# Products that keep TensorE streaming, 64-column relative scores, row norms on ScalarE and a q/k/v scratch with its channels outermost

## What is computed

```
x = x + window_attention(layernorm(x))     # windows of 14x14, 12 heads of 16, relative scores of rows and columns
t = t + experts(layernorm(t))              # softmax router, 2 of 8 experts, 192 -> 768 -> 192, exact gelu
x = x + dilated_attention(layernorm(x))    # 3x3 neighbours at dilations 1, 2 and 3, 4 groups, heads of 16
t = t + experts(layernorm(t))

# in the window attention, with q reshaped to (windows*heads, 14, 14, 16):
rel_h = einsum('bhwc,hkc->bhwk', q, Rh)    # Rh[h, k] depends on the row h inside its window
rel_w = einsum('bhwc,wkc->bhwk', q, Rw)
attn  = softmax(q @ k.T * scale + rel_h[..., None] + rel_w[..., None, :])
```

## Time and profile before

| | us |
|---|---|
| median of 3 runs (927.88 to 931.53) | 928.06 |
| the profiled execution | 926.22 |
| its span, first to last instruction | 924.4 |
| TensorE busy | 761.4 (82%) |
| VectorE, GpSimd, ScalarE busy | 427.2, 367.6, 297.6 |
| mean granted clock | 0.876 |

### The profile page before, as it was taken

The page is one execution under the profiler, slowest core; times in us unless marked ns, Lnnn a source line. Parts: engine busy times, 40 slices in busy tenths (PEclk is TensorE's granted clock), DMA queues, the critical chain, the costliest instruction groups (busy, mean ns, idle before and its releaser), DMA issues.

```text
span 924.4 us, 19239 instructions
## 1 busy us (share of the span) xinstructions
PE 761.4 (82%) x6098; PEld 668.5 (72%) x6099; DVE 427.2 (46%) x1007; ACT 297.6 (32%) x830; POOL 367.6 (40%) x795
## 2 busy tenths in 40 slices
PE   2999999999891999999981648997682799999990
PEld 1787888888680899999971427883672699999990
DVE  7105545557628333333326305998247433333324
ACT  3222545445523333333331330011210233333330
POOL 5753353330211566666640040000040566676640
PEclk9665899999975899999995778999755899999996
DMA  7382565564581111111103159400861111111115
GB/s 215 104 227 71 127 143 125 141 150 88 173 309 62 45 45 50 44 48 50 50 23 137 30 141 275 68 23 23 301 261 64 40 53 47 47 50 49 46 30 204
DMA packets 63186, 96.51 MB, mean 104 GB/s; under 512 B 28551, under 2 KB 46684, under 8 KB 63136
## 3 DMA queue, kind: packets, MB, share of 16 engines
q1 hardware_dynamic: 42208, 59.60, 22.7%
q0 software_dynamic: 20928, 36.25, 13.1%
HBM read 65.51 MB, written 31.52 MB: 105 GB/s over the span
## 4 chain that ended last, share of the span: by engine, by line
PE 64%; DVE 16%; DMA 6%; issue 5%; POOL 4%; ACT 2%; SPq 1%; DVEq 0%; POOLq 0%
PE ps L1367 14%; PE ps L1375 10%; PE ps L1379 6%; PE ps L735 5%; DMA qkvd<-arena 3%; PE ps L717 3%; PE ps L761 3%; DVE x_sb L1316 2%; PE ps L374 2%; PE ps L745 2%; PE ps L1358 2%; PE ps L1764 2%; PE ps L1746 2%; PE ps L781 2%; DVE arena L1660 2%
## 5 line engine op out<-in xcount | busy, mean ns | idle before, releaser
L1409 ACT ACTIVATE arena<-ps,b1s 128x128 f32<-128x128 f32 x468 | 129.5, 376 | 256.9 <-PE ps L1379 254.1
L1367 PE MATMUL ps<-arena 128*128 x936 | 165.4, 327 | 1.5 <-DVE rt L1281 1.5
L1367 PEld LDWEIGHTS ps<-arena 128*128 128x128 f32 x936 | 150.3, 190 | 2.4 <-issue 2.1
L1375 PE MATMUL ps<-xnT 128*128 128x128 f32 x936 | 120.1, 279 | 3.5 <-DVE xnT L1274 3.5
L1375 PEld LDWEIGHTS ps<-xnT 128*128 128x128 f32 x936 | 116.8, 195 | 4.8 <-DVE xnT L1274 4.8
L270 POOL TENSOR_TENSOR rstd<-veps,cst 128x8 f32<-128x8 f32 (+2 forms) x6 | 10.0, 1659 | 205.0 <-DVE veps L264 205.0
L597 DVE TENSOR_REDUCE rt<-ps 98x2 f32<-98x392 f32 x96 | 52.8, 561 | 78.8 <-PE ps L761 78.8
L1423 POOL TENSOR_TENSOR credit<-credit 1x1 f32<-1x1 f32 x306 | 58.1, 190 | 78.0 <-DVE rt L1281 33.4
L1431 POOL DMA_INDIRECT xnT<-xnd,gcur x78 | 79.1, 1014 | 16.3 <-issue 14.9
L1379 PE MATMUL ps<-xnT,rt 64*128 64x128 f32 x936 | 73.7, 290 | 0.0
L983 ACT ACTIVATE arena<-ps 98x392 f32<-98x392 f32 x96 | 46.9, 499 | 78.4 <-PE ps L781 77.7
(11 more groups left out here) (199 smaller groups left out, 1249.8 us busy)
## 6 DMA issues: line engine op xcount, KB each, us to landing
arena<-in_w SPq DMA_DIRECT2D x16, 576.0 KB, 8.6
arena<-in_w1a SPq DMA_DIRECT2D x16, 384.0 KB, 6.3
arena<-yd SPq DMA_DIRECT2D x8, 768.0 KB, 6.8
kk<-kd SPq DMA_DIRECT2D x48, 96.0 KB
qq<-qd SPq DMA_DIRECT2D x16, 264.0 KB
qd<-arena POOLq DMA_DIRECT2D x16, 224.0 KB, 5.3
qq<-qd SPq DMA_DIRECT2D x16, 192.0 KB
arena<-in_w1b SPq DMA_DIRECT2D x16, 192.0 KB, 6.9
```

Source lines behind the costliest of these rows:

```text
L1367: last = mm(ps[:, DOWN, 0:C], hidT[r][:, f, :], w2s[:, e, f, :], start=f == 0, stop=f == FT - 1)
L1375: mm(hidden(r, f), wcura[r][:, f * P:(f + 1) * P], xgT[:, 0, :], start=f < 2, stop=False, skip_group_check=True)
L1409: last = nc.scalar.activation(hidT[r][:, f, :], hidden(r, f), ACT.Gelu, bias=b1s[l][:, bass.ds(e * FT + f, 1)])
```

## The change

1. `relative` makes rows `at` and `at + 14` in one product (`at::WS`): both lie at the same place in their window and use the same weights. 14 products instead of 16, two of them with 64 columns. The pieces of `relative` are now 3, 4, 3 and 4 values of `at`.
2. Products whose results nobody reads are put on TensorE: 9 of 512 columns before the first transposes (on a tile of ones that VectorE fills), 2 before `r2` of block 0, one of 256 columns (16-bit) after each of the 18 steps of `scores_for_max` ahead of the main loop, 6 and 4 of 512 columns around the tables in each routing, 9 before the transposes of the dilated attention's result, and one for each block in the second router.
3. The norms ahead of the dilated attention and of the second MoE go block by block. VectorE makes the moments of block b, then scale and offset of block b - 1 (`block_scales`); ScalarE applies them (`block_normalise`); GpSimd's powers come one for each block.
4. In the second router a block's transposes are directly followed by its own logits.
5. `qkvd` has the channel outermost, the rows of `wqkv1` are permuted to match, and each unit is one store (12 in all, before 18). SyncE's loads come in another order: k of index 2; q and k of index 1, v of index 2; q and k of index 0, v of index 1, v of index 0.
6. In `values` for the later two dilations the single term is made before the pair.

Cut to its core:

```diff
-        qkvd = dram("qkvd", [3 * len(DIL), HD, SPU, GRP, PIX])
+        qkvd = dram("qkvd", [HD, 3 * len(DIL) * SPU, GRP, PIX])
...
+        def block_scales(v, n, b):
+            ln_refine(v, n, range(b, b + 1))
+            nc.vector.scalar_tensor_tensor(offset[:, b], mv[:, b, :, 0], -1.0, rstd[:, b], ALU.mult, ALU.mult)\
+                .then_inc(s_("ln_offset"), 1)
+        def block_normalise(act, n, b):
+            act.wait_ge(s_("ln_offset"), (BLKS if n == 3 else 0) + b + 1)
+            if n == 2 and b >= 2:
+                act.wait_ge(s_("xn_free"), b - 1)
+            for j in range(TPB):
+                last = nc.scalar.activation(normed(n, b)[:, j, :], x_sb[:, b * TPB + j, :], ACT.Identity,
+                                            bias=offset[:, b, j:j + 1], scale=rstd[:, b, j:j + 1])
...
-                for at in range(4 * piece, 4 * piece + 4):
+                for at in PIECES[piece]:
...
-                        last = mm(o[:, :, at, :] if w == 0 else o[:, :, :, at], relt[w][0:rows, at % WS, 0:cols],
-                                  q[:, :, at, :] if w == 0 else q[:, :, :, at], start=True, stop=True)
+                        if w == 0:
+                            o, q = o[:, :, at::WS, :], q[:, :, at::WS, :]
+                        else:
+                            o, q = o[:, :, :, at::WS], q[:, :, :, at::WS]
+                        last = mm(o, relt[w][0:rows, at, 0:cols], q, start=True, stop=True)
...
+            pe.wait_ge(s_("filler_ready"), 1)
+            keep_clock(BANK["r2", 0], 9)
+            pe.wait_ge(s_("cst_in"), 16)
...
+            keep_clock(BANK["r2", 0], 2)
             relatives(0, 2)
...
                     scores_for_max(H, u)
+                    mm(ps[:, PV, 0:2 * P], trib, maskb[:, 0, 0:2 * P], start=True, stop=True)
...
-                nx_transpose(pe, l, 0)
                 for b in range(BLKS):
-                    if b + 1 < BLKS:
-                        nx_transpose(pe, l, b + 1)
+                    nx_transpose(pe, l, b)
+                    mm(ps[:, 5, :], ident, cst[:, 0:BT], start=True, stop=True)
                     router_logits(pe, l, b)
...
             last.then_inc(s_("ranks_mm"), 1)
+            for _ in range(6):
+                mm(ps[:, 0, :], ident, cst[:, 0:BT], start=True, stop=True)
...
             last.then_inc(s_("tables_mm"), 1)
+            for _ in range(4):
+                mm(ps[:, 0, :], ident, cst[:, 0:BT], start=True, stop=True)
...
+            for k in range(STORES):
+                unit, n = STORES * phase + k, ((2 - phase) * STORES + k) * UNIT
                 eng.wait_ge(s_("qkv_staged"), 2 * unit + 2)
-                to = qkvd[lo // SPU, :, lo % SPU:lo % SPU + hi - lo].rearrange("c b g x -> b c (g x)")
-                eng.dma_start(to, stage[row * HD:(row + hi - lo) * HD, unit]).then_inc(s_(f"qkv_out{phase}"), 16)
+                eng.dma_start(qkvd[:, n:n + UNIT].rearrange("c n g x -> c n (g x)"), stage[:, unit])\
+                    .then_inc(s_(f"qkv_out{phase}"), 16)
...
                 for col in range(3):
+                    value_product(i, 3 * col + 2, next_term()).then_inc(s_("pv_term"), 1)
                     a_ = next_term()
...
-                    value_product(i, 3 * col + 2, next_term()).then_inc(s_("pv_term"), 1)
...
+            for _ in range(9):
+                nc.tensor.matmul(ps[:, 4, :], ident, cst[:, 0:BT], start=True, stop=True)
...
+            for b in range(3):
+                copy_values(b)
+            block_normalise(act, 3, 0)
+            copy_values(3)
+            for b in range(BLKS):
+                if b + 1 < BLKS:
+                    block_normalise(act, 3, b + 1)
+                nx_copy(act, 1, b)
```

91 lines of the change are left out of this document (47 added, 44 removed).

## The result

The changed kernel takes 897.63 us (median of 897.03, 897.56, 897.70 and 902.99) against 929.36 before (927.88 to 931.53): ratio 0.967, 95% interval 0.9626 to 0.9713. I had forecast 876, range 862 to 896. The direction was right and the size was not: the profiled execution has 897.03, so 29.2 us less than the 926.22 of before, where I had counted 50.4. The mean clock went from 0.876 to 0.911. (By the sum, 876 was the profiled execution's time; with the 1.8 us that the prediction puts between it and the median it should have said 877.6.)

What follows compares the result with a forecast made beforehand. TensorE bounds the tile loops and main loop; the time lies in half-clock front and second router, and store waits. 10 + 8.5 + 2 + 3.2 + 4 + 15 + 0.7 + 7 = 50.4 off 926.22 gives 875.8, said 876; range 862 to 896.

Steps and rivals of the forecast that it cites:

- Front: Ahead of the main loop: added products help the clock, so the main loop starts 10 us earlier (3 to 14).
- First five heads: Start of the main loop: heads take 13.6 us instead of 22.13, 8.5 us less (2 to 10).
- Relative scores in the main loop: Main loop of the window attention: wider products save 2 us (0.5 to 3).
- Routings and first tiles: Both routings: first tiles run at full clock, 3.2 us less together (4 more to 3.5 less).
- Norm: Before the dilated attention: hidden powers and ScalarE normalising give 4 us less (2 to 5).
- Stores and loads: q, k, v of the dilated attention: stores spread over 16 engines, first sums of index 1 come 15 us earlier.
- four terms (3.3, 10.5, 3.5, 16): Dilated attention, in us: store landing, q and k of index 2 loading, one column of products, TensorE's channel sums; 33.3 together.
- Tail and second router: Behind the dilated attention: the second router's work at full clock gives 7 us less (0 to 11).
- Rival A: All places with added products: they do not hold the clock; gain 24 us, so 902; chance 0.2.
- some of the products work: The half of Rival A in which some added products hold the clock; included in the range 862 to 896.
- Rival D: Filled gaps alone keep full clock, also in relative scores; 866 to 865, at best 862; chance 0.05.
- Rival B: Dilated attention: stores spread but short-piece loads limit, q and k of index 1 8 us later; 884; chance 0.1.

Runs made afterwards that it cites:

- Experiment 1: The changed kernel with SyncE issuing the load of the first negated maxima (nm) ahead of the last chunk's load; 888.11 us, ratio 0.9573.
- experiments 1 to 4, 6 and 7: Here, variants of the changed kernel: nm load moved, waits filled with unread products, routing products removed, or ScalarE's last value copy moved; 883.96 to 901.89 us.
- stores_alone: The kernel before with only the new q/k/v scratch layout, 12 stores and new load order; 912.93 us, ratio 0.9851.
- norms_alone: The kernel before with only the norms by block, applied by ScalarE; 930.07 us, ratio 1.002.
- experiment 4: The changed kernel with seven unread products in the nm wait and two ahead of the wait for GpSimd's query copy, 891.50 us; with the two alone, 892.25 us.
- experiment 3: The kernel of Experiment 1 plus two unread 512-column products ahead of the main loop's wait for GpSimd's copy of the queries; 890.04 us.
- tail_copy_first: nm_and_gap_filled with ScalarE's last copy of attention values (block 3) ahead of the norm of block 0; 883.96 us, again 885.21 us.
- nm_before_last_chunk: The kernel of Experiment 1: the changed kernel with the nm load issued ahead of the last chunk's; 888.11 us.
- nm_and_gap_filled: The kernel of experiment 3: nm_before_last_chunk plus two unread products ahead of the wait for GpSimd's query copy; 890.04 us.
- gap_filled_alone: The changed kernel with only two unread products ahead of the wait for GpSimd's query copy, the nm wait left idle; 892.25 us.
- fill_nm_wait: The changed kernel with seven unread 512-column products in the wait for nm ahead of the main loop; 894.06 us.
- no_routing_fillers: The changed kernel without the six and four unread products in each routing; 901.89 us, ratio 0.9728.
- five_before_r2: tail_copy_first with five instead of two unread products ahead of r2 of block 0; 884.63 us, ratio 0.9552.
- experiment 8: tail_copy_first with five products before r2; with two between r0 and r1 of block 1; with both plus three before the router's first logits: 884.63, 888.85, 884.56 us.

## Why the prediction was wrong where it was, and right where it was

- **Front, 10 counted, 4.3 came.** The failed step is "Main loop starts 10 earlier": I took the maxima's end for the main loop's start. The load of `nm` stands between them, and I had not followed what is in SyncE's queue ahead of it. Experiment 1 shows it: with `nm` ahead, the main loop starts 10.3 us behind the first maximum instead of 16.1.
- **That the maxima were 10.6 us earlier, as my parts said, is luck twice over.** The parts were not met. The nine first products brought nothing: the queries behind them still took 7.01 us for eight records (6.97 before), and the relative scores of block 0 started at 25.74 (25.66 before), where I had said 1.5 earlier. `r2` started 0.8 earlier and not 3, but then took 2.05 us instead of 3.62, where I had counted nothing; the values to the queries of block 1 gave the 4 that I said, and `r0` and `r1` of block 1 gave 4.2 instead of 3. And the two profiled executions lie far apart: eight traces with this front (of the changed kernel and of experiments 1 to 4, 6 and 7) have the maxima at 57.9 to 58.5 (four) or 62.5 to 64.2 (four), and three with the front of before (`before`, `stores_alone`, `norms_alone`) at 65.4 to 68.5. The means are 5.9 us apart, so even up to the maxima 10 was too much.
- **First five heads, 8.5 counted, 0.8 lost.** The failed step was "I take 13.6". That the clock would be high there rested on products ahead of it and on no idle stretch behind them; two such stretches came, 5.3 and 0.9 us. With both filled (experiment 4) the heads take 16.2 us, 6.8 less than the 23.04 of before. So even with the clock held the term was 1.7 too large: TensorE is idle for 1.2 of the first 16 us there, busy for 5.19 of 6 and 9.58 of 10.
- **Relative scores in the main loop, 2 counted, 1.1 came**, in my range of 0.5 to 3.
- **Routings and first tiles, 3.2 counted, 2.5 came**; in the trace without the products they are 3.4 slower. First tile: 1.60 us against 2.93, as said. The four products ran mostly at half clock (eight records in 6.37 and 6.07 us), and the first tile came 0.3 us later behind the ranks in both routings.
- **Norm, 4 counted, 1.6 came**, below my 2. VectorE's chain, from the first addition to the last block's offset (before, to its last tile), lost 5.4 us, near the 5.7 that I had counted. The failed term is ScalarE's. Its four tiles take 1.76 us a block, 0.44 each instead of 0.35, which is 0.4 more. And a wait that I had put at nothing comes ahead of them: the last offset is ready at 505.58, but ScalarE is still at block 2's tiles and block 1's copies, and starts the last block's tiles 1.8 us later.

```profile
504.42 1.86 ACT L321 ACTIVATE xn<-x_sb,offset,rstd 128x192 f32<-128x192 f32 x4 [2.19 <-DVE offset L312]
506.19 1.27 ACT L342 ACTIVATE xnT<-ps 96x392 f32<-96x392 f32 x6
507.35 1.87 ACT L321 ACTIVATE xn<-x_sb,offset,rstd 128x192 f32<-128x192 f32 x4
```

- **Stores and loads, 15 counted, 13.7 came**, and each of its four terms (3.3, 10.5, 3.5, 16) was met within 1 us.
- **Tail and second router, 7 counted, 5.6 came.** The router's blocks are 3.5 us apart, once 4.3 (3.3 said), and the delay of the last projection was 3.1 us (2.9 said), but it then ran at half clock, 4.55 us instead of 2.78, which I had not counted. The nine products ahead of the tail's transposes did not hold the clock: TensorE waited 2.21 us behind them, and the 16 transposes took 3.60 us, as before (3.65).

```profile
631.00:633.00 2.00, 0.00 (x0) 0.00 (x0) 0.00 (x0) 0.00 (x0) 0.00 (x0) 1.00 0.96 290
633.00:635.00 2.00, 1.82 (x9) 1.74 (x10) 0.00 (x0) 0.00 (x0) 0.00 (x0) 0.55 1.05 335
```

- **Rival A** (902: the products do not hold the clock) was near in time and right for two of the places: behind the nine products at the start and the nine in the tail, each followed by an idle stretch, the clock was 0.50 and 0.55. In the second router (654 to 669) and at the first tiles it read 1.00. What I had called half of A, "some of the products work", describes the result, and I had drawn the range's upper end, 896, 1.6 us too low for it.
- **Rival D** (filled gaps alone keep the full clock) fails on block 1's relative scores: in the changed kernel the clock fell to 0.54 (56 to 60 us) with no gap in TensorE's work. **Rival B** does not show: q and k of index 1 held nothing up, as the channel sums of both dilations run without a break.

## What to carry to other kernels

When an engine is sped up, follow the consumer's last operand, not its first: write down what stands ahead of it in its DMA queue, and what is still in flight, since an order that costs little behind slow work can become the limit. Two changes of which neither shows a gain by itself (1.4 and 1.6 us here) can show one together (10.9), so try the second before the first is thrown away. Where work is there to hold a clock, list every idle stretch up to the place where the clock is wanted; one that is left open can take the whole gain. And take landmarks from several traces of one kernel before a difference is believed: the two single traces here gave 10.6 us where the means gave 5.9.

## What the runs showed of the hardware that I had not expected

**Idle stretches of under 2 us were followed by the lower clock.** 1.73 us with next to nothing on TensorE (experiment 1) were followed by 0.50 for about 13 us of busy work, worth 4.5 us (20.75 against the 16.25 of experiment 3, where the stretch was filled and the clock stayed). In `tail_copy_first` a wait of 1.54 us for ScalarE in the second router was followed by this (the clock is the third number from the end), with 1.00 again from 644 on:

```profile
639.00:641.00 2.00, 1.87 (x15) 1.87 (x16) 1.36 (x11) 1.48 (x5) 1.56 (x2) 0.91 1.03 415
641.00:644.00 3.00, 3.00 (x12) 2.38 (x13) 0.20 (x2) 1.77 (x5) 2.53 (x5) 0.50 1.03 409
```

**The same instructions get another clock from one execution to the next.** `nm_before_last_chunk` and `nm_and_gap_filled` are the same up to 70 us. In the first the clock was 0.77 from 26 to 34 us, in block 0's relative scores, and TensorE reached `r2` just as GpSimd had its queries (a wait of 1.01 us); the clock stayed up from 40 to 52, and the maxima started at 58.52. In the second the clock was 1.00 from 26 to 34, so TensorE came early and idled:

```profile
38.87 3.19 PE L750 MATMUL ps<-xnT,arena 64*64 64x64 f32 x56 [4.10 <-POOL xnT L556]
```

```profile
40.00:46.00 6.00, 6.00 (x63) 5.94 (x61) 0.11 (x1) 3.46 (x5) 5.27 (x9) 0.50 0.56 152
46.00:52.00 6.00, 5.32 (x28) 4.83 (x28) 1.34 (x4) 1.18 (x2) 1.96 (x4) 0.50 1.03 249
```

The clock fell and the maxima started at 63.98: the execution that was faster for 8 us was 5.5 behind in the end. `gap_filled_alone` has the same picture (idle for 4.21 us, maxima at 64.17). But the wait ahead of `r2` does not decide it alone. In three traces of about 1 us (0.99 to 1.01) the clock was 1.00 from 40 to 52. In two others, `fill_nm_wait` and `no_routing_fillers`, the wait was 0.98 and 0.94 us, the clock was 0.50 from 46 to 52, and the maxima started at 63.04 and 62.45:

```profile
38.44 2.06 PE L747 MATMUL ps<-xnT,arena 64*64 64x64 f32 x56 [0.94 <-POOL xnT L555]
```

(What I had expected of `five_before_r2` counts `fill_nm_wait` among the traces with a wait of 4.10; it is not one of them.) (The Trainium skill, "TensorE: Matmul & The Clock Gate", "Part 1: The HAM clock gate", says that where the clock changes differs from run to run of one kernel. These traces agree.) Each kernel here is known from four to ten executions that spread over 2 to 12 us, and where two medians are 3 us apart I have not called one better. What decides in an execution which way it goes, and why the closed gaps of experiment 8 left the spread, stays open.
